# An attention and expert-layer kernel: one of four output products moves between two transposes, the other three one place later

## What is computed

```python
q = rmsnorm((h @ q_w.T)...); k = rmsnorm((h @ k_w.T)...); v = h @ v_w.T
q = apply_rope(q, cos, sin); k = apply_rope(k, cos, sin)
scores = einsum('bhqd,bhkd->bhqk', q, k) * scale          # causal mask
attn = einsum('bhqk,bhkd->bhqd', softmax(scores), v)
hidden = hidden + attn @ o_w.T
```

## Time and profile before

| | |
|---|---|
| median of 3 runs | 1435.12 us (1435.06 to 1441.99) |
| profiled execution, its own time | 1443.74 us |
| span of the profiled execution | 1441.9 us |
| TensorE matmul busy | 1271.6 us (88%) |
| VectorE busy | 843.9 us (59%) |
| ScalarE busy | 719.3 us (50%) |
| GpSimd busy | 382.5 us (27%) |
| mean granted TensorE clock | 0.953 |

### The profile page before, as it was taken

How to read it: one execution, slowest core, us unless ns; L and a number is a source line. 1 busy time by engine, 2 the same in 40 slices (tenths; PEclk the granted TensorE clock), 3 DMA queues, 4 the chain that set the end, 5 groups by cost and what they waited for, 6 DMA issues and landing times. The chain is left out here.

```text
span 1441.9 us, 22860 instructions
## 1 busy us (share of the span) xinstructions
PE 1271.6 (88%) x6845; PEld 1026.0 (71%) x6845; DVE 843.9 (59%) x2480; ACT 719.3 (50%) x2290; POOL 382.5 (27%) x545
## 2 busy tenths in 40 slices
PE   1867899999999989979999899998999399999995
PEld 0455767787776767757767787786767289998895
DVE  7667876666886665568767566665543523223231
ACT  6447655555675556466655556554453122233331
POOL 0223121232322222222213132331310223334332
PEclk9888999999999999989999999999999599999998
DMA  3270325441455465627544754765301887887432
GB/s 96 76 274 23 119 101 176 168 163 50 165 147 169 169 195 177 234 93 224 173 163 149 232 179 159 203 220 181 113 23 59 257 316 209 257 242 208 77 61 37
DMA packets 89894, 228.50 MB, mean 158 GB/s; under 512 B 12272, under 2 KB 50032, under 8 KB 79536
## 3 DMA queue, kind: packets, MB, share of 16 engines
q1 hardware_dynamic: 77536, 201.86, 40.0%
q0 software_dynamic: 10848, 24.71, 9.2%
q10 hardware_dynamic: 1392, 0.47, 0.2%
HBM read 146.76 MB, written 80.24 MB: 157 GB/s over the span
## 5 line engine op out<-in xcount | busy, mean ns | idle before, releaser
L537 POOL TENSOR_TENSOR prob<-prob,rtotal 128x128 f32<-128x128 f32 (+2 forms) x192 | 117.0, 614 | 463.1 <-DVE rtotal L1283 436.9
L1277 DVE TENSOR_SCALAR_CACHE_REDUCE prob<-bank,nscale 128x128 f32<-128x128 f32 (+3 forms) x256 | 134.9, 544 | 167.4 <-PE bank L715 167.1
L954 ACT ACTIVATE prob<-prob,bias 128x128 f32<-128x128 f32 (+3 forms) x256 | 144.8, 566 | 155.4 <-DVE prob L1277 154.4
L679 PE MATMUL bank<-w_hi,hT_hi 128*128 128x512 f32 x480 | 175.1, 365 | 15.4 <-DVE rot L1242 15.3
L734 PE MATMUL bank<-pT,v 128*128 128x512 f32 (+3 forms) x512 | 177.2, 448 | 9.4 <-ACT pT L960 8.7
L960 ACT ACTIVATE pT<-bank 128x512 f32<-128x512 f32 (+3 forms) x256 | 104.0, 434 | 140.4 <-PE bank L723 139.8
L679 PE MATMUL bank<-w_hi,hT_lo 128*128 128x512 f32 x480 | 163.4, 340 | 0.0
L679 PE MATMUL bank<-w_lo,hT_hi 128*128 128x512 f32 x480 | 163.3, 340 | 0.0
L1587 PE MATMUL gu<-we,xT_hi 128*128 x624 | 156.9, 333 | 3.5 <-DVE xT_lo L1703 2.7
L514 POOL TENSOR_TENSOR r<-r,rot 128x640 f32<-128x640 f32 x60 | 99.8, 1663 | 188.8 <-DVE rot L1242 188.8
L713 PE MATMUL bank<-kT_hi,qT_hi 128*128 128x128 f32 (+3 forms) x256 | 103.8, 405 | 15.7 <-DVE prob L1277 15.6
(11 more groups left out here) (312 smaller groups left out, 2862.9 us busy)
## 6 DMA issues: line engine op xcount, KB each, us to landing
w_hi<-ws_scratch SPq DMA_DIRECT2D x24, 1024.0 KB, 5.1
w_lo<-ws_scratch SPq DMA_DIRECT2D x24, 1024.0 KB, 7.5
we<-wx_scratch SPq DMA_DIRECT2D x16, 1408.0 KB
we<-wx_scratch SPq DMA_DIRECT2D x16, 768.0 KB
stage<-in_wexp SPq DMA_DIRECT2D x64, 176.0 KB, 2.4
wx_scratch<-ehi SPq DMA_DIRECT2D x64, 176.0 KB, 2.6
wx_scratch<-stage SPq DMA_DIRECT2D x64, 176.0 KB, 2.6
stage<-in_wqkvo SPq DMA_DIRECT2D x40, 256.0 KB, 3.2
```

The source lines that it names most:

```text
L537: nc.gpsimd.tensor_tensor(p, p, rtotal[:, 4 * h + q:4 * h + q + 1].broadcast_to([P, KEYS[q]]), ALU.mult).then_inc(prob_ready, 1)
L679: last = nc.tensor.matmul(o, hT[a][:, k, t * P:(t + 1) * P], wkv(j, c, k) if kv else wq(j, c, k), start=(k == 0 and n == 0), stop=(k == KC ...
L954: nc.scalar.activation(p, p, ACT.Exp, bias=bias[:, 4 * h + q:4 * h + q + 1], scale=-1.0, accum_out=total[:, 4 * h + q:4 * h + q + 1]).then ...
L1277: nc.vector.tensor_scalar(prob[(G * it + h) % (LAG + 1)][:, P_AT[q]:P_AT[q] + KEYS[q]], bank[SC + q % 2][:, 0:KEYS[q]], nscale[it % 2][:, ...
```

## The change

Only the table `FILL` changes. In slot (2, 3) one output product stands where two stood, and `n` comes before it. Tiles 1 and 2 move to the next slots that hold output products, and tile 3 goes into slot (3, 3), between `t` 1 and `t` 2. In the last group there are no steps `t`, and tile 3 stands alone in (3, 3).

```diff
         (2, 2): (('kv', 3),),
-        (2, 3): (('o', 0), ('n', 0), ('o', 1)),
-        (3, 1): (('m', 0), ('o', 2)),
-        (3, 2): (('o', 3),),
-        (3, 3): (('t', 0), ('t', 1), ('t', 2), ('t', 3))}
+        (2, 3): (('n', 0), ('o', 0)),
+        (3, 1): (('m', 0), ('o', 1)),
+        (3, 2): (('o', 2),),
+        (3, 3): (('t', 0), ('t', 1), ('o', 3), ('t', 2), ('t', 3))}
```

## The result

| | before | changed |
|---|---|---|
| median | 1437.7 us (11 runs, 1434.27 to 1445.46) | 1431.16 us (11 runs, 1421.86 to 1433.62) |
| ratio to before | | 0.9943, 95% interval 0.9922 to 0.9963 |
| profiled execution: own time, span, mean granted clock | 1443.74, 1441.9, 0.953 | 1427.62, 1425.8, 0.960 |

By the medians the change makes the kernel 6.5 us faster; the forecast was 15 us. By the ratio the gain is 0.57%, some 8 us. The two profiled executions differ by 16.1 us, though, so half of what separates these two traces, or more, is not the change.

What follows compares the result with a forecast made beforehand. TensorE, busy 1271.6 us of a span of 1441.9, was taken as the bound. Terms 3.9 + 1.2 + 5.0 + 5.0 - 1.2 = 13.9, with the last group 15 us, gave 1420 us from the median; range 1401 to 1437.

Steps and rivals of the forecast that it cites:

- Groups 2, 3, 14 (release from TensorE): At these group ends the moved product covers the transposes' wait of 1.6 us each, less 0.3: 3.9 us won.
- Groups 1, 4, 5, 9 (VectorE behind): VectorE's late maxima make TensorE wait anew before head 3, tile 2, so only part is won: 5.0 us.
- Groups 6, 10, 13 (landing): Waits before the fourth batch of transposes are released by a DMA write's landing that does not move: 0 won.
- Groups 7 and 11: Each waits 0.85 us for the logits before the transposes; 0.6 us won in each, 1.2 us in all.
- Clock: Ends of groups 3, 5, 9 and 14 keep the upper clock, 5.0 us won, less 1.2 for one new fall.
- Norms and weights: Earlier norm seeds, and the output weights' reload issued some 3 us later, were charged nothing.
- The base: The forecast was taken from the median of 1435.1 us, giving 1420, not from the profiled execution, giving 1428.7.
- Rival 1: Landings and VectorE move along, so the whole wait at the group ends is covered: 30 to 35 us, 1402; chance 0.15.
- rival 3: The lead is lost before head 3 and the product delays the fourth batch of transposes: up to 1450; chance 0.09.
- rival 5: In groups with g = 2 the product also stands before the third batch's wait for another bank; small; chance 0.02.
- Rival 2: The product leaves an equal hole in slot (2, 3) before head 3, so the wait only moves: 1432; chance 0.22.
- Rival 4: Transposes do not count as busy for the clock; all eight slow ends keep full clock, doubling 5.0 us: 1415; chance 0.08.

Runs made afterwards that it cites:

- before_e: The kernel before with the expert piece of slot (3, 2) moved to slot (0, 1): 1425.42 us, ratio 0.9930.
- before_r: The kernel before with the first routing product ahead of the first output product of slot (2, 3): 1435.72 us, ratio 0.9990.
- n_first: The kernel before with only `n` put ahead of both output products of slot (2, 3): 1443.22 us, ratio 1.0042.
- the edit that removes the landing: Expert piece of slot (3, 2) moved to slot (0, 1): ratio 0.9930 on the kernel before, 0.9891 on the changed kernel.
- The order experiment: Routing product 1 put ahead of the output product of slot (2, 3): ratio 0.9920 on the changed kernel, 0.9990 on the kernel before.
- after_n: The changed kernel with `n` put back behind the output product of slot (2, 3): 1430.91 us, ratio 0.9953 to the kernel before.
- two_front: The kernel before with `n` first and two output products kept in slot (2, 3), none in (3, 2), tile 3 between the transposes: 1439.34 us, ratio 1.0003.
- after_r: The changed kernel with routing product 1 ahead of the output product of slot (2, 3): 1424.50 us, ratio 0.9920 to the kernel before.

## Where the prediction was right, and where it failed

The direction was right, and most waits moved as forecast. The size was not: 15 us forecast, 6.5 measured by the medians, 7.7 by the means of all executions. The table sets the forecast beside two measurements, each a mean of two traces before against three after: how much shorter TensorE's waits are, and how much shorter the groups are, from the start of one group's output products to the next.

| groups | forecast us | waits shorter by us | groups shorter by us |
|---|---|---|---|
| 1 | 1.7 | 1.6 | 1.4 |
| 2, 3, 14, with the clock of 3 and 14 | 3.9 + 2.5 | 1.6 - 0.1 + 1.6 = 3.0 | 1.8 + 0.5 + 3.0 = 5.3 |
| 4, 5, 9, with the clock of 5 and 9 | 3.3 + 2.5 | 0.4 + 1.4 + 1.3 = 3.1 | 0.2 + 2.6 + 2.5 = 5.3 |
| 7, 11 | 1.2 | 0.0 + 0.1 = 0.1 | -1.1 - 1.4 = -2.5 |
| 6, 8, 10, 12, 13 | 0 | -0.3 + 0.1 - 0.1 - 0.2 + 1.2 = 0.6 | 0.1 + 0.4 + 0.0 - 1.1 + 0.8 = 0.2 |
| last group | 1 | 0.3 | 0.2 |
| new falls of the clock | -1.2 | | in the rows above |
| sum | 15 | 8.7 | 9.8 |

So the waits' part of the forecast, 11.1 us, came out at 8.7, and the clock's part, 3.8 us, at 0.4 over all executions. The 9.8 of the last column still holds 3 to 4 us of luck: in these stretches the traces of the kernel before spent some 46 us at the lower clock, those of the changed one some 37, while over all executions the clock is the same. (0.001 of mean clock is 2.9 us of 1430 at the lower level and costs 1.19, so 9 us cost 3.7.) Another 1.6 us of luck stand behind the last row: both traces of the kernel before fall to the lower clock at its last output products, the changed kernel never does, but `before_e`, `before_r` and `n_first` do not either (15.0 us from there to the routing's last wait, against 16.6).

- **Groups 2, 3, 14 (release from TensorE): right.** All three waits are gone, and the 0.3 us that the forecast took off for VectorE's addition does not show in group 2. In group 3 the lead was lost again 10 us later, and the prediction had not followed it that far: VectorE waits there for GpSimd's reduction of the context's column maxima (below), and TensorE's wait at the start of group 4 grew from 1.27 to 3.47 us (1.34 to 2.71 and 2.97 in the other traces), so this group won nothing in waits.
- **Groups 1, 4, 5, 9 (VectorE behind): right, the new wait as well.** It stands before the scores of head 3, tile 2, released by the maxima. Group 8 has it too, 2.41 us in exchange for 2.69.
- **Groups 6, 10, 13 (landing): right, and confirmed by the edit that removes the landing.** (For groups 8 and 12 the cause was wrong, see that edit, though 8 won nothing either.) ScalarE's idle time grew from 4.74 to 6.12 us, as expected of a release that does not move.
- **Groups 7 and 11: the first step that failed.** The forecast took 1.2 us for the 0.85 us that each would lose before the logits, and did not look at what the product taken from slot (2, 3) had been hiding there. The waits before line 703 went (0.85 and 0.82 us), and the routing's transposes wait 0.77 us more each: nothing is won in waits. Clock was lost on top. Group 11 spends 3.6 us at the lower level in all three traces of the changed kernel and none in the two of the kernel before, and group 7 13.3, 7.1 and 13.4 us against 10. So instead of 1.2 us won, the two groups took 2.5 us longer. The order experiment removed the waits and the fall of group 11.
- **Clock: the second step that failed, and the larger one.** "Groups 3, 5, 9 and 14 show this and lose their wait here: 4 x 1.24 = 5.0", less 1.2 for one new fall: 3.8 us, against 0.4 measured over all executions. At those four ends the clock does stay up in all three traces of the changed kernel. But the fall in group 14 was there in only one of the two traces of the kernel before, with the same wait of 1.60 us. And the changed kernel has new or longer waits of 1.2 to 3.5 us at 350, 574, 653 and 844 us, which brought a fall in one, two, two and three of its three traces, where the forecast charged one fall for all new waits. (In group 8 it stands in place of a fall that the kernel before had.) A cost counted from the falls in a single profile is a sample of one.
- **Norms and weights: right at nothing** for the change as it is: neither VectorE before L1271 nor TensorE before L751 has a new wait. `n_first` and `after_n` show that the order of `n` is not harmless as such.
- **The base.** Taking the forecast from the median and not from the profiled execution was right: its clock of 0.953 made it slow, by 4.8 us against the mean clock.
- **Rivals.** Rival 1 (whole wait covered) and rival 3 (slower) did not come; rival 5 neither. Rival 2 (swallowed, 1432) gave nearly the measured time, 1431.16, and its mechanism is at work in more than half of what was moved: of the 18.4 us gone before line 703, 10.9 are back at three other lines. Rival 4 (the clock by the rule of the Trainium skill, 1415) fell: the ends keep their clock, but the total does not follow.

Still open: why GpSimd's reduction comes so late in group 7, and with it 6 us of waiting at the start of group 8, the largest wait left; and how much of the gain needs the three other products moved (`two_front` mixes that with the order of `n`).

## To carry over

When work is moved to fill a hole, list not only what the hole waits for but also every release that the moved work was covering in its old place, group by group; here two groups of sixteen got their covered wait back at another line, with a fall of the clock on top. Follow the lead until it meets a release that does not move (a landing, another engine's slow step), for there it ends. And before a term is written for the clock, look at several executions: between two profiles of one kernel it moved more time than the change did.

## What the hardware showed that was not expected

GpSimd's reduction over partitions does not start when its input is there. In group 3, of the kernel before and of the changed one, VectorE's maxima (first row of each) and GpSimd's reduction:

```profile
346.31 2.27 DVE L1128 TENSOR_REDUCE camax<-cb 128x16 f32<-128x2048 f32 x1
...
349.99 0.39 POOL L500 PARTITION_ALL_REDUCE camaxall<-camax  x1 [5.77 <-issue]
```

```profile
341.22 2.28 DVE L1128 TENSOR_REDUCE camax<-cb 128x16 f32<-128x2048 f32 x1
...
346.64 0.39 POOL L500 PARTITION_ALL_REDUCE camaxall<-camax  x1 [6.52 <-issue]
```

The input is complete (start plus duration of the first row) 1.4 us before the reduction in the one and 3.1 in the other. What stays is the distance from GpSimd's own instruction before it: 5.7 to 6.5 us in group 3 of all fourteen traces (the record of this instruction is rough, but VectorE goes on right behind it in each). If that distance is what counts, which was not tried by itself, maxima that come earlier win nothing as long as GpSimd's step before them does not. In group 7 the same distance was 5.8 us in one trace (`after_r`) and 8.6 to 11.0 in the other thirteen, and the wait of TensorE at the start of group 8 followed it: 2.17 us in the one, 5.5 to 7.3 in the others.
